# Attention core of a hybrid layer on eight cores: score tiles handled in pairs, one exp over 1024 columns

## The reference

```python
q = (x @ Wq.T).reshape(B, T, 2, nh // 2, hd)        # T = 2048, nh = 16, hd = 64
k = (x @ Wk.T).reshape(B, T, 2, nh // 2, hd)
v = (x @ Wv.T).reshape(B, T, nh // 2, 2 * hd)
q, k = _apply_rotary(_rms_norm(q)), _apply_rotary(_rms_norm(k))
y1 = _causal_attn(q[:, :, 0], k[:, :, 0], v, scale)  # softmax(mask(q k^T * scale)) v
y2 = _causal_attn(q[:, :, 1], k[:, :, 1], v, scale)
y = (y1 - lambda_full * y2).reshape(B, T, D)
return y @ Wproj.T
```

## Time and profile before

| | us |
|---|---|
| median of 2 timed runs | 11805.6 |
| the two runs | 11614.91, 11996.28 |
| profiled execution | 11130.27 |
| its span, slowest core | 11128.6 |
| spans of the eight cores | 11052.1 to 11128.6 |
| PE busy in it | 9095.0 (82%) |
| DVE busy | 4093.3 (37%) |
| ACT busy | 1637.5 (15%) |

### The profile page before, as it was taken

One profiled execution on the slowest core, in us unless ns is written; L12 is line 12 of the kernel. 1 busy time (PEld: TensorE's weight loads), 2 busy tenths in 40 slices (PEclk: granted clock), 3 DMA queues, 4 the chain that ended last, 5 costly groups with the idle time before them and its releaser, 6 DMA issues.

```text
span 11128.6 us, 131829 instructions; the slowest of 8 cores (11052.1 to 11128.6 us)
## 1 busy us (share of the span) xinstructions
PE 9095.0 (82%) x39746; PEld 3699.7 (33%) x39746; DVE 4093.3 (37%) x6357; ACT 1637.5 (15%) x2632; POOL 817.1 (7%) x792
## 2 busy tenths in 40 slices
PE   2832999999999999994535554799999999999998
PEld 1311434333334334341212222333433433333333
DVE  1022343443443344345113333243344344444435
ACT  1110111111111111111113332111111111111110
POOL 0032000000000000000650000000000000000000
PEclk9765999999999999996765556899999999999998
DMA  6114122222122212212220005312122111212221
GB/s 108 23 48 97 31 40 31 33 31 44 29 35 40 35 29 41 34 31 72 65 72 5 5 6 129 64 32 43 29 35 40 31 33 31 44 29 35 40 35 40
DMA packets 444760, 466.09 MB, mean 42 GB/s; under 512 B 166680, under 2 KB 364056, under 8 KB 443816
## 3 DMA queue, kind: packets, MB, share of 16 engines
q0 software_dynamic: 271968, 357.66, 18.3%
q1 hardware_dynamic: 172104, 100.00, 4.0%
HBM read 648.52 MB, written 72.35 MB: 65 GB/s over the span
## 4 chain that ended last, share of the span: by engine, by line
PE 73%; DVE 7%; issue 6%; ACT 5%; POOL 4%; DMA 2%; SPq 1%; DVEq 1%; another core or an unknown queue 1%; ACTq 1%; POOLq 0%
PE P L960 23%; PE P L869 22%; PE P L873 22%; DVE pf L219 5%; POOL pf L219 4%; ACT pbf L219 4%; PE P L1302 2%; DVE pbf L219 2%; DVE stat L219 1%; DMA gspill<-pbf 1%; ACT pf L219 1%; PE P L560 1%; PE P L443 1%; PE P L464 1%
## 5 line engine op out<-in xcount | busy, mean ns | idle before, releaser
L960 PE MATMUL P<-pbf 128*128 128x512 bf16 x11264 | 2903.1, 381 | 428.9 <-DVEq L244 300.0
L869 PE MATMUL P<-pbf 128*128 128x512 bf16 x11264 | 2670.0, 380 | 158.0 <-DMA pbf<-W 157.9
L219 DVE SCALAR_TENSOR_TENSOR pf<-P,pf 128x512 f32<-128x512 f32 (+1 forms) x3104 | 2346.1, 756 | 1109.1 <-PE P L960 776.2
L873 PE MATMUL P<-pbf 128*128 128x512 bf16 x11264 | 2662.3, 379 | 0.0
L219 DVE SCALAR_TENSOR_TENSOR pbf<-P,b_sb,pf 128x512 bf16<-128x512 f32 x1408 | 1057.4, 751 | 3741.8 <-ACTq L244 3741.8
L219 ACT ACTIVATE pf<-P,b_sb 128x512 f32<-128x512 f32 x1408 | 968.1, 688 | 7000.6 <-PE P L873 7000.6
L960 PEld LDWEIGHTS P<-pbf 128*128 128x128 bf16 x11264 | 916.2, 96 | 2388.0 <-issue 1685.8
L869 PEld LDWEIGHTS P<-pbf 128*128 128x128 bf16 x11264 | 1103.9, 98 | 1494.2 <-issue 173.1
L873 PEld LDWEIGHTS P<-pbf 128*128 128x128 bf16 x11264 | 1102.8, 98 | 1331.4 <-issue 4.2
L213 POOL DMA_DIRECT2D pbf<-W x288 | 240.9, 847 | 7727.3 <-PE P L960 7574.6
L219 ACT ACTIVATE pbf<-P 128x512 bf16<-128x512 f32 x800 | 478.1, 598 | 1071.9 <-PE P L1265 490.3
(11 more groups left out here) (82 smaller groups left out, 1560.3 us busy)
## 6 DMA issues: line engine op xcount, KB each, us to landing
pbf<-W POOLq DMA_DIRECT2D x240, 1024.0 KB, 12.6
xspill<-pf POOLq DMA_DIRECT2D x48, 512.0 KB, 4.9
pf<-xspill SPq DMA_DIRECT2D x48, 512.0 KB, 4.7
pbf<-W POOLq DMA_DIRECT2D x48, 512.0 KB, 10.2
pf<-x SPq DMA_DIRECT2D x32, 512.0 KB, 4.5
nspill<-pbf POOLq DMA_DIRECT2D x64, 256.0 KB, 2.4
pf<-cs_tab SPq DMA_DIRECT2D x32, 512.0 KB, 3.7
y<-pf POOLq DMA_DIRECT2D x16, 512.0 KB, 3.0
```

Of the source, the lines that this page charges most:

```text
L219: inst = f(*a, **k)
L869: e.matmul(pa, w1v[:, dk * cw + hk * 128: dk * cw + hk * 128 + 128], xnt[:, dk * T + lt * LT: dk * T + lt * LT + LT], start=(dk == 0), sto ...
L873: inst = e.matmul(pb_, w2v[:, dk * cw + hk * 128: dk * cw + hk * 128 + 128], xnt[:, dk * T + lt * LT: dk * T + lt * LT + LT], start=(dk == ...
L960: inst = e.matmul(ps, hb[:, hk * T + lc * 128: hk * T + lc * 128 + 128], w3v[:, hk * 1024 + dtile * 512: hk * 1024 + dtile * 512 + 512], s ...
```

## The change

Key tiles are taken two at a time. Both matmuls of a pair stand in one operation and write the two halves of one whole PSUM tensor, and pairs alternate between P[2] and P[3]. One activation takes the exp over both halves, 1024 columns, into two neighbouring tiles of E_sb. The counter `sco_i` now counts pairs; a pair's matmuls wait for the exp two pairs before. The first of a group still waits for the value matmuls of the group before. The mask, the value matmuls and the rest are as they were.

```diff
-                    for kt in range(nkt):
-                        ps_s = P[2][:, (sco_i % 2) * 512:(sco_i % 2) * 512 + QT]
-                        def mms(e, kt=kt, qt=qt, ik=ik, off=off, ps_s=ps_s):
-                            return e.matmul(
-                                ps_s,
-                                kT[off:off + HD, ik * T + kt * 128: ik * T + kt * 128 + 128],
-                                qT[off:off + HD, ik * T + qt * QT: ik * T + qt * QT + QT],
-                                start=True, stop=True)
+                    for kt0 in range(0, nkt, 2):
+                        npair = min(2, nkt - kt0)
+                        pp = P[2 + (sco_i % 2)]
+                        def mms(e, kt0=kt0, npair=npair, qt=qt, ik=ik, off=off, pp=pp):
+                            for kk in range(npair):
+                                inst = e.matmul(
+                                    pp[:, kk * 512:kk * 512 + QT],
+                                    kT[off:off + HD, ik * T + (kt0 + kk) * 128: ik * T + (kt0 + kk) * 128 + 128],
+                                    qT[off:off + HD, ik * T + qt * QT: ik * T + qt * QT + QT],
+                                    start=True, stop=True)
+                            return inst
...
-                        if prev is not None and kt == 0:
+                        if prev is not None and kt0 == 0:
                             we.append(("pe", (ph, "ymm") + prev + (NQC - 1,)))
-                        def sev(e, kt=kt, ps_s=ps_s):
-                            return e.activation(E_sb[:, kt * 512:kt * 512 + QT], ps_s, AF.Exp)
+                        def sev(e, kt0=kt0, npair=npair, pp=pp):
+                            if npair == 2 and QT == 512:
+                                return e.activation(E_sb[:, kt0 * 512:kt0 * 512 + 1024],
+                                                    pp[:, 0:1024], AF.Exp)
+                            inst = None
+                            for kk in range(npair):
+                                inst = e.activation(E_sb[:, (kt0 + kk) * 512:(kt0 + kk) * 512 + QT],
+                                                    pp[:, kk * 512:kk * 512 + QT], AF.Exp)
+                            return inst
```

More of the change, by code:

```diff
@@ L1261, in phase_attn_b @@
                     nkt = (qt + 1) * NQC
-                    for kt in range(nkt):
-                        ps_s = P[2][:, (sco_i % 2) * 512:(sco_i % 2) * 512 + QT]
-                        def mms(e, kt=kt, qt=qt, ik=ik, off=off, ps_s=ps_s):
-                            return e.matmul(
-                                ps_s,
-                                kT[off:off + HD, ik * T + kt * 128: ik * T + kt * 128 + 128],
-                                qT[off:off + HD, ik * T + qt * QT: ik * T + qt * QT + QT],
-                                start=True, stop=True)
+                    for kt0 in range(0, nkt, 2):
[9 more added lines that the diff above has]
+                            return inst
                         w = []
-                        if h == 0 and m == 0 and qt == 0 and kt == 0:
+                        if h == 0 and m == 0 and qt == 0 and kt0 == 0:
                             w = [("tlq", (ph, "qT", NDK - 1)),
```

## The result

| | before | with the change |
|---|---|---|
| median of all runs, us | 11540.7 (10 runs) | 11457.8 (11 runs) |
| lowest and highest | 11079.2 and 12021.1 | 10945.2 and 11826.5 |
| profiled execution | 11130.3 | 10947.2 |
| ratio | | 0.9878, 95% interval 0.985 to 0.9907 |

The change made the kernel 1.2% faster. In some executions the cores of a die, or of both, show a lower granted clock, whatever the kernel, which spreads the runs of either kernel over some 900 us (one with the change, not among the eleven, took 23364 us); the ratio compares the others, the lowest runs. Those stand at 11080 and 10945 us, about 135 us apart.

What follows compares the result with a forecast made beforehand. The prediction took expert-block matmuls for two thirds of the span and ScalarE's exps as the attention core's bound while scores are made. Wider exps save 140 us, first exps cost 22: 118 less, 11012 us by the profile, range 10950 to 11900.

Steps and rivals of the forecast that it cites:

- How the numbers follow: Prediction's closing step for the whole kernel: 2% taken as measurable, 0.89 on staying the same, 0.06 faster, 0.05 slower.
- the counterpart of 11012 us: Whole kernel: the profiled execution of 11130.3 us less the forecast 118 us, 1.1% less.
- Price of the wide exp: Attention core: one exp over 1024 columns takes 1025 ns, the middle of 993 and 1057.
- The rival that it saves nothing inside: Attention core: wide exp takes 1196 ns, so only 63 us saved, 11067 us by the profile; chance 0.10.
- the gap between dependent ScalarE instructions: Attention core, between exps: 0.27 us, to be paid once for a pair after the change.
- The first exp of a group: Attention core, group start: first exp waits for two matmuls, 0.45 or 0.23 us later, 22 us more in all.
- TensorE keeps up: Attention core: paired score matmuls stay hidden behind the exps, with a cover of 0.09 us for two pairs.
- the loop: Attention core: exp end to matmul, paired matmuls, matmul end to exp, exp; 2.50 us for two pairs against ScalarE's 2.59.
- The rival that it comes up: Attention core: granted clock rises, value matmuls save 109 us more, 227 in all, 10903 us by the profile; chance 0.12.
- A lower clock in the expert blocks: Expert blocks: whole second block at the slower pace costs 652 us more; half gives 11338 us; chance 0.05.
- the forecast of 11688: Whole kernel in terms of the median of two timed runs: 11805.6 us less 118 us.
- The rule against merging: Attention core: skill rule favouring broken-up instructions, judged not to apply within a group, only at its first pair, 22 us.

Runs made afterwards that it cites:

- the kernel with two operations: Changed kernel with each pair's wide exp split into two exps over 512 columns, each an operation with its own wait and increment; core 990 to 993 us.
- the run without the gap: Changed kernel with wide exps that do not wait for the exp before and increment the semaphore themselves; core 793 to 795 us, one whole execution 10959.1 us.
- two pairs ahead: Changed kernel with the next group's first two pairs of score matmuls put before this group's value matmuls; core 818 us, lowest whole execution 10923.4 us.

## Why the prediction was right or wrong

**The sum was right, its reading was not.** 118 us less was forecast for the profiled execution, the core shows 129, and the lowest runs 135 (the ratio's interval on 11080 us is 103 to 166). By terms, on the core: the exps gave 144 us where 140 were forecast, the first exps cost 18 where 22 were, and the value matmuls, put at nothing, gave 3. The step that failed is the last, "How the numbers follow": the text took 2% as what a measurement of this kernel can tell from no change, and so put 0.89 on "no change" for a saving that its own sum gave as 1.1%. The lowest runs of a kernel agree within 2 us (11079.2, 11080.1 and 11081.2 before; 10945.2 and 10945.3 after), and the ratio came with an interval of 0.6% in width: 0.9878 is clear of 1. A saving of 1.1%, whose terms all had one sign but for 22 us, was a forecast of "faster", and should have been given as that. The three times of before that I had, 11130 to 11996, were read as noise on one number; all three were above the 11080 at which the lowest runs agree, and the profiled one by the stretches at 0.81. That is also why the counterpart of 11012 us came out at 10947.2, just below the range of 10950 to 11900: 54 of the 65 us are those stretches, 11 the terms above.

**Price of the wide exp.** Forecast 1025 ns, measured 1025. That it hit to the nanosecond is luck: it was the middle of two bounds, 993 and 1057, without a reason for the middle. The rival that it saves nothing inside (1196) is out. The saving of 140 us is shown by itself, as 138: 991 to 853 us between the kernel with two operations and the changed one.

**What that saving is made of.** I had put down 0.27 us a pair to "the gap between dependent ScalarE instructions". The runs split it: 0.09 us for the wait on the instruction before, 0.18 for the end and start of an operation. The sum was the same, since the change removes both.

**The first exp of a group.** Forecast 22 us more, 1.36 a pass; measured 1.10 a pass, 18 us. The single terms held: 0.81 + 0.43 = 1.24 at the lower clock, 0.59 + 0.22 = 0.81 at the upper. The prediction took half the groups at each clock; 24 of the 64 waited the full 1.24 us (core 4).

**The exps' stretch** gave 0.23 us a pass more than worked out, 4 us in all, and the value matmuls 0.17, 3 us. With the 4 us of the first exp these are the 11 us between 118 and 129. Most of the excess in the exps are single longer gaps, of up to 0.6 us: 17 steps before and 8 after are over 0.05 us longer than the usual one, 4.8 and 2.2 us in all. What makes them is not known.

**TensorE keeps up**: right. ScalarE waited for a score matmul 64 times and not 320, and the run without the gap shows the loop right behind, at 2.28 us for two pairs. With one PSUM tensor the change would have lost.

**The clock.** The rival that it comes up was answered in part: it went from 0.58 to 0.63, but over the value matmuls only 3 us came of it, because most of the time at the upper level (135 of 214 us on core 4) lies where ScalarE sets the pace. A rise of the clock is worth something only where TensorE is on the chain.

**A lower clock in the expert blocks** did not come in the profiled execution with the change, which had 0.99 to 1.00 in both blocks on all cores. Its price was sized too low: the rival set projections against other matmuls and got 17%, but the same projection took 68.5 us at 0.79 and 56.2 at 0.97, 22% more. By the median the forecast of 11688 is 230 us above the measured 11457.8, since the median of two runs that were both far above the lowest was no base to subtract from. The Trainium skill, TensorE: Matmul & The Clock Gate, in its note on a peak-current limiter, has a die go to 13/16 of the clock once three of its cores run dense matmuls. The prediction called that contradicted by the 1.00 in the expert blocks, which does not follow if the cores of a die did not run them at the same time, and the traces hold no common clock to tell. A sign that they did not: three stretches at 0.81 of core 4 before (70, 140 and 85 us, from 10469, 10630 and 10783 us) repeat three of core 7 (68, 137 and 82 us, from 210, 374 and 527 us), each about 10257 us later, as if two pairs of cores had run that far apart and met only there. This is a reading of the rows and not shown by a run.

**The rule against merging**, of the Trainium skill, Perfetto Trace Analysis, section Optimizing Scalar/DVE Operations, says that breaking up instructions may help where ScalarE is not saturated but causes bubbles elsewhere. This case goes the other way: at 39% busy, ScalarE gained from wider instructions, since it was the bound in its own stretch. What merging costs did show too, as the 18 us of the first exp.

## What to carry to other kernels

An engine that is 39% busy over a stage can still set its pace: read the step from one instruction to the next inside the stage, split it into the instruction, the wait for the one before and the waits and increments between operations (here 0.60, 0.09 and 0.18 us), and count how often each is paid. Before widening a consumer, work out the loop that feeds it with its buffers; here a second PSUM tensor was the difference between 129 us gained and 143 lost. And set a small sum against how well the lowest runs of a kernel agree, not against the spread of all runs.

## What the runs showed of the hardware that I had not expected

An exp over 512 columns that nothing waits for starts 0.49 us after the one before, though each shows 0.60 us; over 1024 columns it is 0.92 against 1.02. Waiting for it costs that overlap of 0.11 us and 0.09 more.

TensorE's clock stayed mostly at the lower level in every version of the core, also where score and value matmuls followed one another and TensorE was busy for 76% of it (granted 0.55), and where its gaps were shorter (two pairs ahead: 278 us of gaps, one of them over 3 us, at 0.56; the change alone: 375 us, 64 over 3 us, at 0.63). The score matmuls use 64 of 128 rows; whether that is the reason, no run tells.
